# First attention by whole images, with scores on two 64-row halves of TensorE

## What is computed

```python
qh, kh, vh = heads(q @ mq_w + mq_b), heads(k @ mk_w + mk_b), heads(v @ mv_w + mv_b)  # 8 heads of 16
attn = softmax(einsum('bnqd,bnkd->bnqk', qh, kh))      # per image: 256 queries, 64 sampled keys
att = einsum('bnqk,bnkd->bnqd', attn, vh)              # back to 256 x 128
z = att @ mo_w + mo_b + x
z_ln = layernorm(z)
out = gelu(z_ln @ mlp_w + mlp_b) + z                   # goes into the second layer
```

## Time and profile before

| | us |
|---|---|
| median of 3 runs | 79.7 |
| lowest, highest | 79.41, 115.36 |
| the profiled execution | 79.27 |
| its span, first to last instruction | 77.4 |
| TensorE busy in the span (matmul) | 70.6 |
| VectorE, ScalarE, GpSimd busy | 51.7, 33.9, 24.3 |

### The profile page before, as it was taken

How to read it: one execution, slowest core, us unless ns; L and a number is a source line. 1 busy time by engine, 2 the same in 40 slices (tenths; PEclk the granted TensorE clock), 3 DMA queues, 4 the chain that set the end, 5 groups by cost and what they waited for, 6 DMA issues and landing times.

```text
span 77.4 us, 1968 instructions
## 1 busy us (share of the span) xinstructions
PE 70.6 (91%) x732; PEld 53.6 (69%) x732; DVE 51.7 (67%) x172; ACT 33.9 (44%) x84; POOL 24.3 (31%) x37
## 2 busy tenths in 40 slices
PE   4999699998999999999999999998897999998950
PEld 2345599783786647879777989845485869996830
DVE  0478742116366959477789968599799786868480
ACT  6112397068139563524424419820248048263600
POOL 5008999900000038390019137123820030000000
PEclk9999999999999999999999999999999999999999
DMA  0789870000000000000000000000000000010112
GB/s 9 226 270 150 305 289 12 0 8 0 0 8 0 0 0 4 0 0 8 0 0 0 4 0 0 8 0 0 0 0 0 0 0 4 0 68 9 59 55 89
DMA packets 3051, 3.07 MB, mean 40 GB/s; under 512 B 225, under 2 KB 2657, under 8 KB 3042
## 3 DMA queue, kind: packets, MB, share of 16 engines
q1 hardware_dynamic: 3042, 2.95, 12.8%
HBM read 2.42 MB, written 0.52 MB: 38 GB/s over the span
## 4 chain that ended last, share of the span: by engine, by line
PE 63%; DVE 17%; issue 5%; DMA 5%; ACT 3%; SPq 2%; POOL 2%; DVEq 0%; POOLq 0%; ACTq 0%
PE bank L810 53%; DMA x_hw<-x 5%; PE bank L971 5%; PE bank L1140 2%; DVE smax L604 2%; DVE x_t L656 1%; DVE gst L694 1%; SPq L247 1%; DVE st L528 1%; DVE bilin L578 1%; DVE x_gn L716 1%; DVE dist_y L562 1%; PE bank L989 1%; DVE q_conv L517 1%; POOL grs L330 1%
## 5 line engine op out<-in xcount | busy, mean ns | idle before, releaser
L810 PE MATMUL bank<-k_blk,qh 128*128 128x512 f32 x16 | 8.4, 605 | 0.0
L810 PE MATMUL bank<-v_blk,p_t 128*128 128x34 f32 x64 | 7.8, 267 | 0.0
L810 PEld LDWEIGHTS bank<-v_blk,p_t 128*128 128x128 f32 x64 | 7.8, 192 | 0.0
L810 PE MATMUL bank<-warm 128*128 128x512 bf16 x18 | 6.3, 471 | 1.0 <-POOL warm L269 1.0
L604 DVE TENSOR_REDUCE smax<-bank 128x8 f32<-128x512 f32 x8 | 5.5, 685 | 2.4 <-PE bank L810 2.4
L317 POOL TENSOR_TENSOR zrs<-zve,neg_half 128x2 f32<-128x2 f32 x4 | 2.9, 714 | 12.7 <-DVE zve L646 12.7
L810 PE MATMUL bank<-q_ph,wd 128*32 128x112 f32 (+5 forms) x256 | 6.8, 249 | 0.0
L303 POOL TENSOR_TENSOR x_res<-x_st,msa_bias 128x1024 f32<-128x1024 f32 x1 | 2.4, 2358 | 12.8 <-DVE bilin L578 12.8
L431 ACT ACTIVATE p_t<-bank 128x512 f32<-128x512 f32 x8 | 4.8, 597 | 3.4 <-PE bank L971 3.4
L810 PEld LDWEIGHTS bank<-q_ph,wd 128*32 128x32 f32 x256 | 5.6, 109 | 0.7 <-issue 0.3
L611 DVE TENSOR_TENSOR s_sub<-bank,smax 128x512 f32<-128x512 f32 x8 | 5.5, 682 | 0.1
(11 more groups left out here) (149 smaller groups left out, 161.2 us busy)
## 6 DMA issues: line engine op xcount, KB each, us to landing
x_st<-x SPq DMA_DIRECT2D x1, 512.0 KB, 6.7
pack_late<-late SPq DMA_DIRECT2D x1, 448.0 KB, 7.3
out<-y SPq DMA_DIRECT2D x3, 128.0 KB, 1.7
pack_fold<-fold SPq DMA_DIRECT2D x1, 320.0 KB, 4.1
pack_mid<-mid SPq DMA_DIRECT2D x1, 261.0 KB, 5.8
x_hw<-x SPq DMA_DIRECT2D x2, 128.0 KB, 2.2
x_hw<-x SPq DMA_DIRECT2D x1, 256.0 KB, 3.8
pack_early<-early SPq DMA_DIRECT2D x1, 184.0 KB, 2.5
```

Source lines behind the costliest of these rows:

```text
L810: return pe.matmul(o, l, r_, start=start, stop=stop, **k)
```

## The change

Before, a score product uses all 128 rows of the array with 512 columns. After, heads 0 to 3 (channels 0 to 63) and heads 4 to 7 (channels 64 to 127) are two products of 64 rows and 256 columns with a key block half as wide, and go to bank 3 and bank 4. Those two banks now hold both tiles of an image. From there on:

- the maximum and the shift are one instruction an image over both banks (1024 elements a partition) for images 1 to 3; for image 0 the maximum goes tile by tile and the shift by tile and half
- the values of both tiles go to bank 6; reciprocal, norm, the copy of the transposed attention, and the addition to z are one instruction an image
- the scores of image b + 1 wait for the shift of image b; the transposes of an image's second tile wait for the norm of the image before
- PE's list is written out by image; `z_transpose(0)` and `z_transpose(1)` come behind the last value tile (before: the one ahead of the transposes of tile 7, the other ahead of value tile 7)
- z_hat of images 0 and 1 is made on GpSimd (`z_norm`), of images 2 and 3 on VectorE as before; GpSimd scales its weights ahead of the first `z_scale`
- the key blocks of images 2 and 3 on GpSimd are half as wide.

```diff
-    "mid": [("mo_w", C), ("head_of", NH), ...
+    "mid": [("mo_w", C), ("head_of", NH // 2), ...
+        low = [ctx.enter_context(nc.psum_tensor(f"bank{i}", [P, 512], F32)) for i in range(3)]
+        heads = ctx.enter_context(nc.psum_tensor("heads", [P, 2, 512], F32))
+        high = [ctx.enter_context(nc.psum_tensor(f"bank{i}", [P, 512], F32)) for i in range(5, 8)]
+        bank = low + [heads[:, 0], heads[:, 1]] + high
...
+        def shifted(b, t):
+            return t + 1 if b == 0 else b + S
...
-            z_scale(0)
+            def z_norm(b):
+                pool.wait_ge(s["zrs_ok"], b + 1)
+                for i in (2 * b, 2 * b + 1):
+                    pool.tensor_scalar(z_hat[:, i], z[:, i], zmv[:, i, 0:1], zrs[:, i:i + 1], ALU.subtract, ALU.mult).then_inc(s["zhat_p"], 1)
...
+            z_scale(0)
+            z_norm(0)
             z_scale(1)
+            z_norm(1)
             residual(0)
             residual(1)
...
+            exp_tile(4)
+            exp_tile(5)
+            att_image(1)
+            exp_tile(6)
+            exp_tile(7)
+            att_image(2)
             act.wait_ge(s["outbias_mm"], 1)
             act.copy(out_bias[:, :], bank[7][:, 0:C]).then_inc(s["outbias_ok"], 1)
-            exp_tile(T - 1)
-            att_tile(T - 3)
             zt_image(0)
             act.activation(scratch[:, 3:4], eps[:, :], ACT.Gelu)
             zt_image(1)
-            att_tile(T - 2)
             act.wait_ge(s["cols1_ok"], 3)
             gelu_image(0)
+            att_image(3)
             gelu_image(1)
-            att_tile(T - 1)
...
+            def max_heads(b):
+                dve.wait_ge(s["s_mm"], 4 * b + 4)
+                dve.tensor_reduce(smax[:, b % 2].rearrange("p r t h -> p (r t h)"), heads[:, :, :].rearrange("p r (n q) -> p (r n) q", q=PIX),
+                                  AX.X, ALU.max).then_inc(s["smax_ok"], 1)
+            def shift_heads(b):
+                dve.wait_ge(s["smax_ok"], b + S)
+                if b >= 2:
+                    dve.wait_ge(s["pt_mm"], 2 * (b - 1))
+                dve.tensor_tensor(s_sub[:, b % 2].rearrange("p r t h q -> p (r t h) q"), heads[:, :, :].rearrange("p r (n q) -> p (r n) q", q=PIX),
+                                  smax[:, b % 2].rearrange("p r t h -> p (r t h)").unsqueeze(2).to_broadcast([P, 2 * NH, PIX]),
+                                  ALU.subtract).then_inc(s["ssub_ok"], 1)
...
             max_tile(0)
             shift_tile(0)
             rows_apart(1)
+            max_tile(1)
+            shift_tile(1)
+            sample_weights(1)
+            bilinear(1)
+            max_heads(1)
+            sample_out(1)
+            shift_heads(1)
+            recip_image(0)
+            norm_att(0)
+            value_half(dve.tensor_copy, dve, 0, 1, s["v_even"])
+            max_heads(2)
+            shift_heads(2)
+            recip_image(1)
+            norm_att(1)
+            z_image(0)
+            z_norm_stats(0)
+            max_heads(3)
+            shift_heads(3)
+            recip_image(2)
+            norm_att(2)
+            z_image(1)
+            z_norm_stats(1)
...
+            recip_image(3)
+            norm_att(3)
+            z_image(2)
+            z_norm_stats(2)
             x1_image(0)
-            z_tile(T - 2)
             x1_image(1)
             gn_stats(0)
             gn_stats(1)
-            z_tile(T - 1)
+            z_image(3)
             gn_aggr(0)
             gn_aggr(1)
+            z_norm_stats(3)
...
-            def score_tile(i):
...
-                mm(bank[3 + i % 2][:, :], qh[:, i * P:(i + 1) * P], k_blk[:, b].rearrange("p h q -> p (h q)")).then_inc(s["s_mm"], 1)
+            def score_heads(b):
...
+                if b >= 1:
+                    pe.wait_ge(s["ssub_ok"], shifted(b - 1, S - 1))
+                for t in range(S):
+                    i = 2 * b + t
+                    for r_ in range(2):
+                        h = slice(r_ * P // 2, (r_ + 1) * P // 2)
+                        mm(bank[3 + r_][:, t * HW:(t + 1) * HW], qh[h, i * P:(i + 1) * P],
+                           k_blk[h, b].rearrange("p h q -> p (h q)")).then_inc(s["s_mm"], 1)
...
             conv_half(1, 8, N)
-            score_tile(0)
+            score_heads(0)
             coord_half(1)
-            score_tile(1)
             residual_bias()
             query_half(1)
+            transpose_scores(0)
+            transpose_scores(1)
+            score_heads(1)
+            sample_half(1)
+            value_tile(0)
+            value_tile(1)
+            key_half(1)
+            transpose_scores(2)
+            att_transpose(0)
+            transpose_scores(3)
+            score_heads(2)
+            value_tile(2)
+            out_project(0)
+            value_tile(3)
+            fold_second()
+            transpose_scores(4)
+            att_transpose(1)
+            transpose_scores(5)
+            score_heads(3)
+            value_tile(4)
+            out_project(1)
+            value_tile(5)
+            transpose_scores(6)
+            att_transpose(2)
+            transpose_scores(7)
...
+            value_tile(6)
+            out_project(2)
+            value_tile(7)
+            z_transpose(0)
             z_transpose(1)
-            value_tile(T - 1)
-            att_transpose(T - 2)
+            att_transpose(3)
             mlp_image(0)
             mlp_image(1)
-            out_project(T - 2)
-            att_transpose(T - 1)
+            out_project(3)
             keep_warm(2, 6)
-            out_project(T - 1)
             gelu_transpose(0)
             gelu_transpose(1)
...
-        "head_of": (p[:, None] // HD == np.arange(NH)[None, :]).astype(f32),
+        "head_of": (p[:, None] // HD % (NH // 2) == np.arange(NH // 2)[None, :]).astype(f32),
```

More of the change, by code:

```diff
@@ L186, in build @@
             "attention": """s_mm smax_ok ssub_ok pt_mm exp_ok av_mm recip_ok att_ok attt_mm attt_ok msa_mm xres_ok z_ok""",
-            "norm of z and MLP": "zst_ok zmv_ok zve_ok zrs_ok zhat_ok zt_mm zt_ok mlp_mm gel_ok zres_ok x1t_ok gelt_mm x1res_ok",
+            "norm of z and MLP": "zst_ok zmv_ok zve_ok zrs_ok zhat_ok zhat_p zt_mm zt_ok mlp_mm gel_ok zres_ok x1t_ok gelt_mm x1res_ok",
             "group norm": "gst_ok gmv_ok dev_mm dev2_ok gvar_mm gve_ok gmean_ok grs_ok xgn_ok",
@@ L431, in exp_tile, with att_image @@
                 act.activation(p_t[:, i % 2].rearrange("p j q -> p (j q)"), bank[5 + i % 2][:, :], ACT.Exp).then_inc(s["exp_ok"], 1)
[L433 to L438, removed]
+            def att_image(b):
+                act.wait_ge(s["attt_mm"], b + 1)
+                if b >= 2:
+                    act.wait_ge(s["msa_mm"], b - 1)
+                act.copy(att_t[:, b % 2].rearrange("p s q -> p (s q)"), bank[0][:, 0:HW]).then_inc(s["attt_ok"], 1)
             def zt_image(b):
@@ L446, in gelu_image @@
                 act.activation(gel_t[:, b], bank[3 + b][:, 0:HW], ACT.Gelu, bias=cols1[:, 2:3]).then_inc(s["gel_ok"], 1)
[L448 to L458, removed]
+            exp_tile(0)
+            query_out()
+            exp_tile(1)
+            key_out()
+            value_half(act.copy, act, 1, 1, s["v_odd"])
+            exp_tile(2)
+            exp_tile(3)
+            att_image(0)
+            fold_out()
+            exp_tile(4)
[4 more added lines that the diff above has]
+            att_image(2)
             act.wait_ge(s["outbias_mm"], 1)
             act.copy(out_bias[:, :], bank[7][:, 0:C]).then_inc(s["outbias_ok"], 1)
-            exp_tile(T - 1)
-            att_tile(T - 3)
             zt_image(0)
@@ L614, in av, with max_tile @@
[L614 to L628, removed]
+            def max_tile(t):
+                dve.wait_ge(s["s_mm"], 4)
+                dve.tensor_reduce(smax[:, 0, :, t], heads[:, :, :].rearrange("p r (t h q) -> p r t h q", t=S, h=NH // 2)[:, :, t],
+                                  AX.X, ALU.max).then_inc(s["smax_ok"], 1)
@@ new lines, in av_view, with recip_image, norm_att @@
+            def av_view():
+                return bank[6][:, 0:S * PAIRS * VW].rearrange("p (n d) -> p n d", d=VW)
+            def recip_image(b):
+                dve.wait_ge(s["av_mm"], 2 * b + 2)
+                dve.reciprocal(recip[:, b % 2].rearrange("p (n e) -> p n e", e=2), av_view()[:, :, 2 * HD:VW]).then_inc(s["recip_ok"], 1)
+            def norm_att(b):
+                dve.wait_ge(s["recip_ok"], b + 1)
+                if b >= 2:
+                    dve.wait_ge(s["attt_mm"], b - 1)
+                dve.tensor_tensor(att[:, b % 2].rearrange("p t (j e d) -> p (t j) e d", j=PAIRS, e=2),
+                                  av_view()[:, :, 0:2 * HD].rearrange("p n (e d) -> p n e d", e=2),
+                                  recip[:, b % 2].rearrange("p (n e) -> p n e", e=2).unsqueeze(3).to_broadcast([P, S * PAIRS, 2, HD]),
@@ L662, in x1_residual, with z_norm_stats @@
                                   z_res[:, 2 * b:2 * b + 2], ALU.add).then_inc(s["x1res_ok"], 1)
```

(29 more changed lines are left out.)

166 lines of the change are left out of this document (64 added, 102 removed).

## The result

The change made the kernel slower: 80.16 us (median of 20 runs, 79.54 to 86.79) against 79.34 for the kernel before in the same comparison, a ratio of 1.010 with a 95% interval of 1.0075 to 1.0126. Forecast was 78.9, inside "within 2%" but on the other side of no change. A second comparison of the same program gave 1.0037 (1.0005 to 1.0069). The two point to losses of 0.8 and 0.3 us, and their intervals do not overlap, so one series alone doesn't tell the size. The profiled execution had a span of 78.1, against 77.4.

The account below looks back on a forecast made before the run. TensorE's queue was taken to bound the first attention; image 1's statistics were to come at 51.4 instead of 52.0, so 79.5 - 0.6 = 78.9 us. Forecast's own range 78.4 to 79.3, eight in ten 77.6 to 80.9.

Parts of the forecast that it names:

- within 2%: Outcome class for the whole kernel: time between 77.9 and 81.1 us, neither faster nor slower by 1.6 us; chance 0.60.
- from the copy to the statistics: Tail, from ScalarE's copy of z of image 0 to image 1's statistics: about 0.2 shorter than 4.80, less 0.15.
- what the scores cost: TensorE, first attention: one image's scores take 0.2 + 0.85 + 0.2 = 1.25 us against 1.72, a gain of 0.47.
- Rivals 1: TensorE scores: row halves take turns, 1.71 us an image, 3.4 later in all, time 82.3; chance 0.10.
- rival 2: TensorE scores: weight loads don't overlap products of their own half, 1.28 us an image, 1.7 later, 80.6; chance 0.10.
- VectorE on 1024 elements: First attention on VectorE: maximum and shift take 1.22 us each, 2.44 an image; upper bound 2.74.
- the pieces of the loop: First attention, images 0 to 3: TensorE and VectorE durations summed from scores at 22.69 to the last shift's end at 41.82.
- the way from the last shift to the copy: Tail on TensorE: from 41.86 through values, projection and z transposes to 46.62; ScalarE's copy of z begins at 46.79.
- Everything behind is the same program: After image 1's statistics, at 51.4 instead of 52.0: the rest of the kernel is unchanged.
- the place of z of image 0: Tail on TensorE: z of image 0 now stands behind the last two value tiles, giving back most of the gain there.
- z_hat on GpSimd: Images 0 and 1, costs nothing: 0.61 us an instruction, image 1 ready about 45.3, wanted at 46.6, cover 1.3.
- number 4: TensorE-VectorE loop dominates: wide VectorE operations +0.3 an image, hand-overs 0.1 late, some 0.6 in all, 79.5; chance 0.20.

## Why the prediction failed

Forecast was a gain of 0.6, measured a loss of 0.69 from the first scores on. The step that failed is the sum over the loop and the tail: its durations were too short by 0.55 up to the last shift, by 0.30 from there to the copy, by 0.16 from the copy to the statistics, and a gap of 0.37 at the end was not in it; some 0.06 came back on the way. The copy of z of image 0 began at 47.60, beyond the 47.2 that the prediction named as a sign of being wrong, and value tile 7 ended at 46.93 for 46.2.

**Right: what the scores cost.** 1.25 an image was said, of which 1.05 to the next line; 1.07 is shown. The records start in pairs, one of each half, less than 0.01 apart. Rivals 1 (halves in turn) and 2 (loads uncovered) fall, and with rival 2 the rule of the Trainium skill (TensorE: Matmul & The Clock Gate, The mechanism) as I had read it: 1.5 to the next line did not come. The prediction names the section after the one that has the rule. The Trainium skill (TensorEngine Tiling (Array Packing), Key Properties) has the array drained at a change of tiling mode; the trace agrees in so far as there is a pause of 0.1 on either side.

**Right: VectorE on 1024 elements**, 1.22 each as the slope gave:

```profile
34.42 1.23 DVE L630 TENSOR_REDUCE smax<-heads 128x16 f32<-128x1024 f32 x1 [2.05 <-PE heads L832]
35.68 1.22 DVE L638 TENSOR_TENSOR s_sub<-heads,smax 128x1024 f32<-128x1024 f32 x1
```

**Wrong, 0.55: the pieces of the loop.** The last shift was said to end at 19.13, it ended at 19.68. The order of waits was as written: TensorE set the steps of images 1 and 2, and the loop of both engines that of image 3. Each stretch was too short: by 0.09 up to the transposes of tile 1, then by 0.23, 0.11 and 0.12 in images 1, 2 and 3.

The largest part, 0.23, is in places where TensorE never stood still. Durations had been read where a piece stands behind transposes, and the new list puts it behind value products of 34 columns. `fold_second` before, then after:

```profile
34.42 0.27 PE L989 MATMUL bank<-pack_early,att 128*128 128x128 f32 x1
34.53 0.39 PE L810 MATMUL bank<-pack_late 128*128 128x128 f32 x2
34.75 0.73 PE L810 MATMUL bank<-pack_early,pack_late 128*128 128x1 f32 x6
```

```profile
35.72 0.98 PE L832 MATMUL bank<-v_blk,p_t 128*128 128x34 f32 x8
36.53 0.47 PE L832 MATMUL bank<-pack_late 128*128 128x128 f32 x2
36.84 0.73 PE L832 MATMUL bank<-pack_early,pack_late 128*128 128x1 f32 x6
```

The same two products take 0.31 for 0.22. So `fold_second` took 0.89 for 0.81, `key_half` 0.78 for 0.71, and two value tiles in a row 1.80 for 1.72. The rows had this price: the output projection behind a value tile took 0.31, and the sum used it there and nowhere else. The rest is small: transposes to scores after a wait took 0.59 for 0.53 (27.11 to 27.70), and from the first score product to the maximum it took 1.21 where 1.12 was said (0.1, 0.85 and 0.17), which counts in images 0 and 3, where the path goes over VectorE.

**Wrong, 0.30: the way from the last shift to the copy.** 4.97 was said, 5.27 shown. From the shift to the attention transposes of image 2 it took 0.68 for 0.56, and these 0.28 for 0.22, since TensorE had waited for VectorE ahead of them. Value tile 6 and the transposes of z each took some 0.05 more.

**Wrong, 0.16: from the copy to the statistics.** "About 0.2 shorter" than 4.80 was wrong; it took 4.77. GELU 0 did begin sooner behind the copy (2.05 for 2.58 before), but GELU 1 waits for the second MLP product, which stood still for 1.03 until the second copy had come, and so it began 2.94 behind the first copy, as before (2.96).

**Missed, 0.37: the end.** "Everything behind is the same program" holds for the list of instructions, not for where they stand in the stream. Nothing in the trace of before shows this price.

**Right and not used: the place of z of image 0.** The prediction names it as the point where the gain is given back, and takes it as fixed. The runs show that it is the lever: of the 1.1 us won by the loop, the table load's place alone holds 1.0.

**z_hat on GpSimd** took 0.79 an instruction, not the 0.61 of the scaling of weights. For image 1 it was ready at 46.70 instead of 45.3, and its transposes began at 47.62. It was not in the way, as "at no cost" said.

```profile
45.12 1.58 POOL L343 TENSOR_SCALAR z_hat<-z,zmv,zrs 128x128 f32<-128x128 f32 x2
```

Of the rivals, number 4 came nearest: it gave 0.6 back to hand-overs that come late by up to 0.1 each, and the first two wrong steps are 0.85. Its other half, VectorE at the upper bound, was wrong, and hand-overs are the smaller part of what was late.

## What to carry to other kernels

Where a faster loop hands over to a tail, draw the tail of every engine again: here one line of ScalarE's list, a table load behind a copy instead of in front of it, held nearly all that TensorE had gained. Take the price of a piece from a place where the same kind of work stands ahead of it: 0.08 us here and 0.06 there, in many places, made a forecast gain of 0.6 nothing. When two lists differ, compare them where the same work has been done, or work that was only moved looks like a gain. And count from an event that both kernels share: starts that scatter by 1 us hide differences behind them that repeat to 0.01.

## What the hardware showed

- Two 64-row halves with 256 columns each run fully side by side: eight records give way after 1.07. The pairs follow each other every 0.22, so 0.86 of this is work and the rest the open first load and the pause. The full array takes 1.72 for the same scores.
- Two fp32 products of 128 columns take 0.31 behind products of 34 columns and 0.22 behind transposes, in an array that never stands still.
- VectorE's last reciprocal started 0.36 later or not, with the same data, by its place in the engine's stream: late with 152 recorded instructions in the whole program, not late with 150, 156, 158 and, in the kernel before, 172.
- A tensor-by-two-scalars operation of 128 x 128 on GpSimd takes 0.79 where the one with one scalar takes 0.61.
- From the first scores to the last shift eleven traces of the new loop agree to 0.01 us, while the first scores themselves started between 22.32 and 23.35.
